# Down's adapter in the empty rows of the last k tile, single transposes of x, and builds spread over the products

## The reference

```python
# layer 0: a quantised linear layer with a low-rank correction
lora_delta = lora_B @ lora_A * (32 / 64)
wg = (weight + lora_delta) in groups of 128;  normalized = wg / exp(scale_log)
quantized = nearest level of the codebook (8 levels)
w_eff = quantized * scale + lora_delta
x = x + x @ w_eff.T
# layer 1: gated MLP, F = 2752, each projection with its sequence's own rank-16 adapter
gate = x @ W_gate.T + adapter;  up = x @ W_up.T + adapter
act = silu(gate) * up
down = act @ W_down.T + (act @ A_down[i].T) @ B_down[i].T * 0.5
x = x + down
```

## Time and profile before

| | |
|---|---|
| median of 3 runs | 1664.09 us |
| the profiled execution's own time | 1666.95 us |
| its span, first to last instruction | 1665.1 us |
| PE busy | 1615.3 us, 7200 matmuls |
| DVE busy | 1286.9 us |
| ACT busy | 567.5 us |
| mean granted TensorE clock | 0.992 |

### The profile page before, as it was taken

One profiled execution on the slowest core, in us unless ns is written; L12 is line 12 of the kernel. 1 busy time (PEld: TensorE's weight loads), 2 busy tenths in 40 slices (PEclk: granted clock), 3 DMA queues, 4 the chain that ended last, 5 costly groups with the idle time before them and its releaser, 6 DMA issues.

```text
span 1665.1 us, 21694 instructions
## 1 busy us (share of the span) xinstructions
PE 1615.3 (97%) x7200; PEld 1322.0 (79%) x7200; DVE 1286.9 (77%) x1736; ACT 567.5 (34%) x1007; POOL 522.4 (31%) x399
## 2 busy tenths in 40 slices
PE   6799999999999999988999999999999899999999
PEld 5688887888888888766878888888777788888887
DVE  6699969888888999987788998998675566785342
ACT  5411125433333333353333333333342333233231
POOL 3230011455655555633434555555310000000000
PEclk9999999999999999999999999999999999999999
DMA  9472265466667777692446777876369667676453
GB/s 275 90 141 86 80 181 138 112 162 159 166 159 164 178 184 177 165 282 62 115 116 138 177 181 182 181 179 150 92 187 244 146 182 185 148 217 198 150 173 106
DMA packets 382830, 266.80 MB, mean 160 GB/s; under 512 B 228608, under 2 KB 303360, under 8 KB 382592
## 3 DMA queue, kind: packets, MB, share of 16 engines
q1 hardware_dynamic: 300640, 232.20, 54.0%
q10 hardware_dynamic: 80000, 27.41, 6.9%
q0 software_dynamic: 2080, 5.80, 1.8%
HBM read 169.41 MB, written 90.14 MB: 156 GB/s over the span
## 4 chain that ended last, share of the span: by engine, by line
PE 87%; DVE 7%; DMA 3%; issue 1%; ACTq 1%; ACT 1%; SPq 0%; DVEq 0%
PE bank L1697 19%; PE bankA L1697 13%; PE bankC L1697 13%; PE bank L1934 9%; PE bankA L1934 6%; PE bankC L1934 6%; PE bank L1835 5%; PE bankT L1835 4%; PE bankT L1934 3%; PE bankT L1744 1%; PE bankT L1745 1%; DVE xl L1221 1%; PE bankC L1709 1%; ACTq L1010 1%; DMA at<-AT_d 1%
## 5 line engine op out<-in xcount | busy, mean ns | idle before, releaser
L922 ACT CAST rh<-wt 128x512 fp32r<-128x512 f32 (+1 forms) x308 | 188.2, 611 | 446.6 <-PE bankA L1709 100.6
L1212 DVE TENSOR_TENSOR rl<-wt,rh 128x512 fp32r<-128x512 f32 (+1 forms) x308 | 281.7, 920 | 6.7 <-ACT rh L922 6.6
L1374 DVE TENSOR_TENSOR ll<-ll,lh 128x512 fp32r<-128x512 f32 (+1 forms) x154 | 108.0, 704 | 172.0 <-ACT lh L1022 171.9
L1697 PE MATMUL bank<-xh,rl 128*128 128x512 f32 (+1 forms) x528 | 205.7, 390 | 0.0
L1697 PE MATMUL bank<-xl,rh 128*128 128x512 f32 (+1 forms) x528 | 205.7, 389 | 0.0
L1697 PE MATMUL bank<-xh,rh 128*128 128x512 f32 (+1 forms) x528 | 205.6, 389 | 0.0
L1022 ACT CAST lh<-ll 128x512 fp32r<-128x512 f32 (+1 forms) x154 | 94.9, 620 | 292.5 <-DMA ll<-LT_d 180.7
L789 POOL TENSOR_TENSOR wt<-wt 128x512 f32<-128x512 f32 (+1 forms) x44 | 57.5, 1307 | 320.9 <-DVE wt L1206 320.9
L1697 PE MATMUL bankC<-xh,rh 128*128 128x512 f32 (+1 forms) x352 | 137.1, 390 | 1.9 <-issue 1.9
L1697 PE MATMUL bankC<-xh,rl 128*128 128x512 f32 (+1 forms) x352 | 137.1, 390 | 0.0
L1697 PE MATMUL bankA<-xh,rl 128*128 128x512 f32 (+1 forms) x352 | 137.1, 390 | 0.0
(11 more groups left out here) (220 smaller groups left out, 3643.2 us busy)
## 6 DMA issues: line engine op xcount, KB each, us to landing
ll<-LT_d SPq DMA_DIRECT2D x140, 256.0 KB, 2.9
wn<-in_L_cond_W_gate_dram SPq DMA_DIRECT2D x80, 256.0 KB, 5.5
wn<-in_L_cond_W_up_dram SPq DMA_DIRECT2D x80, 256.0 KB, 5.1
RT_d<-dt SPq DMA_DIRECT2D x70, 256.0 KB, 3.1
ql<-RT_d SPq DMA_DIRECT2D x70, 256.0 KB, 3.9
LT_d<-ev ACTq DMA_DIRECT2D x60, 256.0 KB, 2.9
dn<-in_L_cond_W_down_dram SPq DMA_DIRECT2D x86, 128.0 KB, 3.9
LT_d<-s2a SPq DMA_DIRECT2D x40, 256.0 KB, 4.1
```

The lines of the kernel that those rows point to most:

```text
L922: nc.scalar.copy(rh[:, v % RING, 0:KH * rows], wsrc(RSRC[p], rows)).then_inc(s_hi, 1)
L1212: dv.tensor_tensor(rl[:, v % RING, 0:KH * rows], wsrc(RSRC[p], rows), rh[:, v % RING, 0:KH * rows].bitcast(f32), ALU.subtract).then_inc(s_ ...
L1374: dv.tensor_tensor(ll[0:rows, n % NL, :], ll[0:rows, n % NL, :].bitcast(f32), lh[0:rows, n % NL, :].bitcast(f32), ALU.subtract).then_inc(s ...
L1697: last = te.matmul(OUT[p][0:rows, :], a[:, u % RING, cols], b[:, OPND[p], k, :], start=k == 0 and n == 0, stop=k == KH - 1 and n == 2 and ...
```

## The change

1. Block 2: the rank-32 adapter term of a token chunk is put into rows 96 to 127 of the last k tile of products M2, M3, M7 and M4 (`ADAPT`). `store_td` stores the masked td_s there (LT_d), `load_rb` loads the matching 32 rows of B_down's transpose (BdT_d, or BdX_d, a difference of its halves made once on VectorE) for each half of the tokens; the second half's rows are split by `rb_hi` and `rb_lo`. The matmuls at line 1939, td2, bd, bdn, TD_d and td_mk are gone.
2. Part 1: x pieces are transposed once; the minus matmul is added to the same bank (four banks in turn). 16 steps stand ahead of the first product, 16 among the first two.
3. Part 1: the order of the products is by o; build o is done after k step `BUILD[o]` counted over all products (16, 47, 78, ..., 202), adapters and lora_B eight k steps later. SP and ScalarE follow.
4. Prologue: lora_A is loaded first, the first weight tile by ScalarE's queue; the first splits of lora_A and lora_B are made on VectorE; the exponential is ahead of the first x copy.
5. B_down's transpose is stored once, unsplit (no bd_lo).
6. Block 1: the mask is applied inside `ts_hi` and `ts_lo` (8 instructions of half the columns in place of 4, the two multiplies of `ts_sum` gone); `load_at(1, 0)` is issued four products earlier; in the second half's first products td comes one product later; `ad_lo` of each half's last tile stands earlier on VectorE.
7. Block 2: `load_res` is spread over three steps (3, 3 and 2 DMAs).

```diff
-                BdT_d = [2, BR, D];  TD_d = [NC, P, CH]
+                BdT_d = [BR, D];     BdX_d = [BR, CH]
+        bankX = [bankW[0], bankM, bankW[1], bankL]
+        def bank_of(u):
+            return bankX[u % 4 if u < XFIRST else (1, 3, 0, 2)[u % 4]]
-        XFIRST = 3 * KD
+        XFIRST = 2 * KD
-        ORDER = [(0, 0), (0, 1)]
-        for o in range(1, KD - 1):
-            ORDER += [(o, 0), (o, 1), (o - 1, 2), (o - 1, 3)]
-        ORDER += [(KD - 1, 0), (KD - 1, 1), (KD - 2, 2), (KD - 1, 2), (KD - 2, 3), (KD - 1, 3)]
+        ORDER = [(o, c) for o in range(KD - 2) for c in range(NC)]
+        ORDER += [(KD - 2, 0), (KD - 2, 1), (KD - 1, 0), (KD - 1, 1)]
+        ORDER += [(KD - 2, 2), (KD - 1, 2), (KD - 2, 3), (KD - 1, 3)]
+        BUILD = {o: 2 * KD + 31 * (o - 1) for o in range(1, KD)}
+        LATER = KD
...
+        ADAPT = {M2: (0, 0), M3: (0, 1), M7: (1, 1), M4: (1, None)}
...
 store_td (SP)
-                        sp.dma_start(TD_d[2 * h + t, :, :], td_mk[t][:, :].bitcast(f32)).then_inc(s_tdst, 16)
+                        for prod in ((M2, M3), (M7, M4))[t]:
+                            sp.dma_start(LT_d[prod, h, NJ - 1, FH:P, :], td_s[2 * t * CR:(2 * t + 1) * CR, :]).then_inc(s_tdst, 16)
...
+                def load_rb(pi, h, signal):
+                    t, half = ADAPT[PORD[pi]]
+                    c = 2 * h + t
+                    if half is None:
+                        sp.wait_ge(s_bxst, 16)
+                        src = BdX_d[c * CR:(c + 1) * CR, :]
+                    else:
+                        sp.wait_ge(s_bdst, 16 * KD)
+                        src = BdT_d[c * CR:(c + 1) * CR, half * CH:(half + 1) * CH]
+                    if h == 1:
+                        step_done(sp, NJ * (2 * pi + 1) - 1)
+                    sp.dma_start(ql[FH:P, NJ - 1, :].bitcast(f32), src).then_inc(signal, 16)
...
 block 2 on SP
-                    if n in (9, 12, 15, 18):
-                        sp.dma_start(bd[i * CR:(i + 1) * CR, :, :].bitcast(f32), BdT_d[i // 2]...)
-                    if n == 19:
-                        sp.dma_start(td2[:, :, :].bitcast(f32), TD_d.rearrange("c p n -> p c n")).then_inc(s_td, 16)
+                    if r % 2 == 1 and k == 1 and PORD[r // 2] in ADAPT:
+                        load_rb(r // 2, 1, s_rb)
+                    if n == 17:
+                        for half in range(2):
+                            sp.dma_start(bdx[:, half, :], BdT_d[:, half * CH:(half + 1) * CH]).then_inc(s_bdl, 16)
+                    if n == 26:
+                        sp.dma_start(BdX_d[:, :], bdx[:, 2, :]).then_inc(s_bxst, 16)
...
 ts_hi (ScalarE), ts_lo (VectorE)
-                        ins = nc.scalar.copy(ts[i * CR:(i + 1) * CR, t, i % 2, :], tx[i % 2 * CR:(i % 2 + 1) * CR, :])
+                        for b in range(CB):
+                            part = slice(b * SEQ, (b + 1) * SEQ)
+                            ins = nc.scalar.activation(ts[i * CR:(i + 1) * CR, t, i % 2, part], tx[g, part], ACT.Copy,
+                                                       scale=half_of[g, b:b + 1])
...
+                def rb_hi(pi):
+                    act.wait_ge(s_rb, ...)
+                    nc.scalar.copy(qh[FH:P, NJ - 1, :], ql[FH:P, NJ - 1, :].bitcast(f32)).then_inc(s_rbh, 1)
...
 block 2 on ScalarE
-                    if n % 3 == 0 and n // 3 < len(RES):
-                        load_res(n // 3)
+                    if r % 2 == 1 and k == 4 and PORD[r // 2] in ADAPT:
+                        rb_hi(r // 2)
+                    if n // 3 < len(RES):
+                        load_res(n // 3, n % 3)
...
 TensorE, part 1
-                    for tt in range(TT):
-                        te.matmul(bankN[u % 2][:, tt * P:(tt + 1) * P], nat_tile(u, tt), ident[:, :],
-                                  is_transpose=True, start=tt == 0, stop=False)
-                    te.matmul(bankN[u % 2], minus[:, :], lxh[c][:, k, :], start=False, stop=True).then_inc(s_neg, 1)
+                def nat_minus(u):
+                    pe.wait_ge(s_hiX, u + 1)
+                    te.matmul(bank_of(u), minus[:, :], lxh[u // KD][:, u % KD, :], start=False, stop=True,
+                              skip_group_check=True).then_inc(s_neg, 1)
...
 main(i), behind k step k, g = i * KD + k
+                        if XFIRST + g < NX:
+                            if XFIRST + g + 2 < NX:
+                                nat_group(XFIRST + g + 2)
+                            nat_minus(XFIRST + g)
+                        for o_ in range(1, KD):
+                            if g == BUILD[o_]:
+                                if o_ + 1 < KD:
+                                    lora_delta(o_ + 1)
+                                w_groups(o_)
+                            if g == BUILD[o_] + LATER:
+                                if o_ + 2 < KD:
+                                    lb_group(o_ + 2)
+                                adapters_tr(o_ - 1)
...
 TensorE, block 2
-                        if k == NJ - 1:
-                            for i, (b, c, half) in enumerate(adds):
-                                w = bdn[:, h, :] if b is bdn else bd[:, c, half * CH:(half + 1) * CH]
-                                last = te.matmul(out_, td2[:, c, tok], w, start=False, stop=i == len(adds) - 1)
+                    if h == 1 and k == NJ - 1 and prod in ADAPT:
+                        pe.wait_ge(s_rbl, sum(p_ in ADAPT for p_ in PORD[:r // 2 + 1]))
```

More of the change, by code:

```diff
@@ L320, in cond_resid_kernel, with k_rows, r_count @@
         assert xs_at + 2 * TILE <= ev_at and xl_at + (NL + NJ + 8) * TILE <= xh_at and ring_at + 8 * TILE <= wn_at and wn_at + 8 * TILE <= base + S0 + 40960
-        td2 = over("td2", [P, NC, CH], f32r, ts_at)
-        bd = over("bd", [P, NC, D], f32r, ev_at)
-        bdn = over("bdn", [P, 2, CH], f32r, ah_at)
+        bdx = over("bdx", [P, 3, CH], f32, ev_at)
+        ADAPT = {M2: (0, 0), M3: (0, 1), M7: (1, 1), M4: (1, None)}
+        def k_rows(prod, k):
+            return P if prod in ADAPT else rows_of(k)
+        def r_count(pi, k):
+            return 16 * sum(2 if k == NJ - 1 and prod in ADAPT else 1 for prod in PORD[:pi + 1])
         BANK2 = [[bank1[:, :], bankA[:, 0, :], bankA[:, 1, :], bank7[:, :]],
@@ L1002, in silu, with load_res @@
                     nc.scalar.activation(ev[r, 0, q, :], ev[r, 0, q, :], ACT.Silu).then_inc(s_sg, 1)
[L1004 removed]
+                def load_res(n, part):
                     q, h, t = RES[n]
[L1006 to L1008 removed]
+                    if part == 0:
+                        wait(act, s_res, n - 1)
+                    for ge in ((0, 1, 2), (3, 4, 5), (6, 7))[part]:
+                            g, e = ge // 2, ge % 2
                             i = 2 * (q % 2) + e
@@ L1316, in ts_lo @@
                         g = (i + 1) % 2
-                        ins = dv.tensor_tensor(ts[block[i], t, g, :], tx[block[g], :], ts[block[g], t, g, :].bitcast(f32),
-                                               ALU.subtract)
+                        for b in range(CB):
+                            part = slice(b * SEQ, (b + 1) * SEQ)
+                            ins = dv.scalar_tensor_tensor(out=ts[block[i], t, g, part], in0=tx[block[g], part],
+                                                          scalar=half_of[block[g], b:b + 1],
+                                                          in1=ts[block[g], t, g, part].bitcast(f32),
+                                                          op0=ALU.mult, op1=ALU.subtract)
                     ins.then_inc(s_ts, 1)
@@ L1363, in dve_tail, with rb_lo @@
                             a_lo(4 * (it - 1) + q + 1)
+                def rb_lo(pi):
+                    dve.wait_ge(s_rbh, sum(prod in ADAPT for prod in PORD[:pi + 1]))
+                    dv.tensor_tensor(ql[FH:P, NJ - 1, :], ql[FH:P, NJ - 1, :].bitcast(f32), qh[FH:P, NJ - 1, :].bitcast(f32),
+                                     ALU.subtract).then_inc(s_rbl, 1)
                 def r_lo(pi, k):
-                    rows = rows_of(k)
+                    rows = k_rows(PORD[pi], k)
                     dve.wait_ge(s_rh, NJ * pi + k + 1)
@@ L1584, in _ @@
                             w_tr(v // 7, n)
+                    if m == 1 and p == 6 and it % NJ == NJ - 1:
+                        ad_lo(it)
                     if mm in (0, NM // 2) and p == 3:
@@ L1614, in _ @@
                                          an[:, :, :, :].rearrange("p f t r -> p (f t r)")).then_inc(s_ar, 1)
-                        if p == 6:
-                            dve.wait_ge(s_adh, it + 1)
-                            for t in range(2):
-                                ins = dv.tensor_tensor(ad[:, :, t, t, 1, :], ar[:, :, t, :], ad[:, :, t, t, 0, :].bitcast(f32),
-                                                       ALU.subtract)
-                            ins.then_inc(s_ad, 1)
+                        if p == 6 and it % NJ != NJ - 1:
+                            ad_lo(it)
```

333 lines of the change are left out of this document (153 added, 180 removed).

## The result

The changed kernel takes 1641.7 us (median of 4 runs, 1641.4 to 1646.6) against 1664.8 for the one before (median of 4: a run of 1668.2 has joined the three above); the ratio is 0.988, with a 95% interval of 0.986 to 0.991. The forecast was 1637, with 1624 to 1649 as its range; by the medians the change is worth 23.1 us, where 27.2 were forecast.

| stage, us | before | after | forecast | measured |
|---|---|---|---|---|
| to the first product | 53.2 | 46.2 | -7.0 | -7.0 |
| products of part 1 | 209.7 | 206.8 | -4.8 | -2.9 |
| start of block 1 (to the product behind the second ts) | 40.6 | 47.7 | +2.0 | +7.2 |
| rest of its first half | 417.7 | 418.0 | 0 | +0.2 |
| middle (second set of x) | 82.7 | 82.0 | -0.7 | -0.7 |

The account below looks back on a forecast made before the run. TensorE, busy 97% of the span, was taken as the bound, with few waits and half-clock matmuls behind them. Terms -11.8 + 2.0 - 0.7 - 9.1 - 8.1 + 0.5 = -27.2 us gave 1637 from the median 1664.09; range 1624 to 1649.

Parts of the forecast that it names:

- its own signs: Stated failure tests: part 1 ending outside 247 to 256, block 2 not 16 to 18 us shorter, new waits in block 1's stream.
- The first product: Start of part 1: x steps end near 35, some 5 us wait for eff, first product at 46.2, 7.0 us earlier.
- The products of part 1: First product to part 1's end: 204.9 us instead of 209.65, builds at 23.8 us on VectorE, end at 251.1.
- the +3.0 for eff: Later builds of part 1: eff late by 0.4 to 0.5 us, six times, +3.0 us (bounds 0 and 6).
- Part 2: Into block 1: later x1 reload +0.5, halved masked sums +1.5, together +2.0 us (bounds 0 and 4).
- Part 3: Second set of x, 720 to 802 us: earlier T(1), later second ts, together -0.7 us (bounds -7 and +3).
- The rest of block 1: Block 1 outside its start and middle: stream left untouched, forecast 0; new waits there would prove the prediction wrong.
- Block 2: 40 matmuls fewer, -9.1 us; the 5.3 us stall and its half clock gone, -8.1; +0.5 for what is left.
- the 0.5 kept for what is left: Block 2: +0.5 us allowed for what remains after the stall's -8.1.
- Rival C: Block 2: the stall stays because xs's small transfers, not bd, are the load; 1645 us, chance 0.09.
- rival B: Part 1 turns VectorE or clock bound: eff later (+3), half clock through 16 mixed steps (+3); 1643 us, chance 0.17.

Follow-up runs that it names:

- e9: The changed kernel repeated with no edit, to show the spread between executions; median 1640.7 us, 0.986 of the kernel before.
- e1_mask: Changed kernel with the mask applied as before: two VectorE multiplies on the sum, then four copies and four subtracts of 512 columns; 1632.4 us, 0.984 of the kernel before.
- e8_stores_early: Changed kernel with SyncE's two adapter stores of o = 6 ahead of the store of the first product of o = 7; 1638.2 us, 0.986 of the kernel before.
- e11: Changed kernel with old mask, o = 6 stores ahead, GpSimd's gathers in three groups, 24 x steps before the first product; 1626.0 us, 0.977 of the kernel before.
- e12: The edits of e11 on the changed kernel, but 20 x steps ahead instead of 24 and the codebook under its own semaphore; 1622.8 us, 0.976 of the kernel before.
- e7: The kernel before the change, with only the xs loads of a residual spread over three steps (3, 3 and 2); 1655.8 us, 0.996 of the kernel before.
- e10_td_work: Changed kernel with two copies and two subtracts of 32x512 put back on VectorE in each make_td, into unread rows; 1643.4 us, 0.988 of the kernel before.
- e6: Changed kernel with the eight xs loads of a residual issued in one step again, every third step; 1641.0 us, 0.987 of the kernel before.
- e3: Changed kernel with GpSimd's last 24 gathers issued in three groups of 8, each after a quantisation's compare-and-scale steps; 1638.0 us, 0.987 of the kernel before.
- e2: Changed kernel with SyncE's two adapter stores of o = 6 moved behind the first two reloads of x1; 1643.8 us, 0.991 of the kernel before.

## Why the prediction was right, and where its terms were off

The time lies within the range, and the four savings that carry the sum came: an earlier first product, no wait for lwl behind it, 40 matmuls fewer and no stall in block 2. How near the sum came is in part luck, as the terms show. By its own signs the prediction held for part 1 (252.9 is within 247 to 256) and failed narrowly for block 2, which got 18.8 us shorter and not 16 to 18.

- **The first product.** 46.19 against 46.2. That it fits to a hundredth is chance: with nothing changed before it, it came at 44.7 to 46.3 in other runs. Nor was every step right: TensorE ended its x steps at 31.4 and not at 35 (0.98 us each, from 15.7 on), so its new wait was 9.3 us and not 5. VectorE's chain set the product, and that was worked out right.
- **The products of part 1.** The pace of 23.8 us a build was nearly right, but not by its sum: 22.6 - 0.2 + 1.2 is 23.6. The quantisation takes the 22.4 of that sum and VectorE's wait for the correction 1.46, not 1.2, together 23.9. The 0.4 to 0.5 us of lateness were right in kind: three builds wait 0.2. The term that was off is the +3.0 for eff: 3.9 in five builds, with a half clock of 3.4 us behind the first, since two builds were slowed by GpSimd's gathers. The forecast took its 22.6 us for a quantisation from one that no gather touched. That this half clock is there is not the rule (e9 has none). And 251.1 against 252.9 is within the spread: the runs that leave part 1 alone end at 251.5 in the mean.
- **Part 2** failed in size. "Together +2.0 (bounds 0 and 4)" was +7.2, outside its bounds, and so it is in every run that leaves this stage alone (+5.2 to +8.2). Three things were mis-sized: the halves were charged once and as 1.5, while they stand in two sums, 0.9 in the first and 1.9 in the second, where ScalarE's and VectorE's shares add; the reload was 1.1 later, not 0.5; and nothing was charged for the clock, though the prediction's own first paragraph says that a wait costs its length and the matmuls behind it. The adapter matmuls lost 1.6 and the product behind the second ts 1.1; the first loss is in all these runs in some size, the second in four of nine. e1_mask shows the halves, e8_stores_early the reload, and with both undone (e11, e12) the two waits are 1.8 and 0.5, as before the change. The stage is still 1.6 longer than before there: half clock stands behind the 1.8 us, and behind the same wait before the change it did not.
- **Part 3** came out at -0.7 by luck. The stage is 82.0 in the profiled execution, but 82.0 to 85.3 in the nine runs that leave it alone, 83.6 in the mean, and the kernel before has 82.7 and, in e7, 80.0. So whether the change wins anything here isn't shown. What failed is the cost of the halves, at least 3.1 us (e1_mask), where I had +0.6 and, for the later second ts, +1.5. Without them the stage is 78.9, 1.1 to 3.8 below before: something of the earlier load_at and ad_lo and the moved td is worth that, and which was not tried.
- **The rest of block 1** I "left untouched". The kernel before had lost 2.4 us at four places in td's matmuls; two stand right behind the td_mk steps, whose going I had costed nowhere. e10_td_work brings 2.0 back. The two small ones (0.2 and 0.5) need not be the change's: in e7, whose block 1 is that of before, they are 0 and 0.2.
- **Block 2.** The 40 matmuls are worth their 9.1 by count (40 x 0.227); no run has them alone. The stall was worth 9.2 and not 8.1: the waits of 5.4 and 0.7 and 3.1 of slow matmuls; and the 0.5 kept for what is left wasn't needed. Rival C's "xs's small transfers are the load" is refuted by e6. The rule of the Trainium skill, page "DMA: Bandwidth & Descriptors", section "Issuing engines are not separate DMA queues", says that an issue from elsewhere saves only the issue's time. The trace of e7 agrees in that a stall remains while the traffic does (3.5 us); e7's median, 6.3 us below before, says that the splitting may have been worth more than issue time.
- The Trainium skill's page "VectorE: DVE Perf Modes", section "The TRN2 errata", was right to speak against the halving. VectorE's eight halves took 0.44 us each, 3.53 in all, near the estimate of 0.424 by that page, against 0.69 for a whole one. The rule was weighed in the prediction and then charged too low.

The errors of +1.9 and +5.2 stand against -2.6 and -2.1, so the sum missed by 2.5 of 27; that they have opposite signs is luck. By the medians it missed by 4.1, and 1641.7 is nearer to rival B's 1643 than to 1637, but not for B's reason: B had 6 us more in part 1, where 1.9 came; the excess lies at the start of block 1.

## What to carry to other kernels

A fixed cost per instruction is paid in each turn of the chain that the instruction stands in, and by each engine where they take turns: count the places and the engines before halving a tile to save another step. A new wait is to be charged with slow matmuls behind it, as a range: behind waits of 3.8 us and more at the start of block 1 the half clock came each time, behind one of 2.5 in four runs of nine, behind one of 1.8 in e11 and e12 but not in the kernel before. Work that is removed far from the place of the change, on an engine that is 78% busy, is to be looked up too: which of TensorE's small waits stand behind it?

## What the runs showed of the hardware

- While GpSimd issues gathers, VectorE's tensor_scalar on 128x1024 takes 1.41 us instead of 0.81, and 1.58 at worst; its tensor_tensor of the same size keeps its 1.22 (e3, at 83.43 and 85.17 us). The Trainium skill, page "SBUF — State Buffer", section "Who interferes with whom", says that tensor_scalar, in its 2-port modes, takes a port pair shared with GpSimd, and that who comes second is blocked for the whole instruction. Which operation slowed agrees; that the ports are the reason no run here shows. A step grew by 0.6 us, not by the 4.4 us that eight issues take.
- In two executions of the same kernel two stages differ by 3 us in opposite directions (part 1 252.9 and 249.6, the middle 82.0 and 84.9), so that a span alone shows neither.
- A store of 64 KB behind two reloads of 1 MB landed after 8.8 us (e2), ahead of them after 4.2 (the changed kernel) and 2.2 (e8).
